# A chunked state-space layer: the state update as three f16 products, and two TensorE steps issued one projection tile later

## The reference, cut to what matters

```python
proj = einsum('bld,pd->blp', hidden_states, in_proj_w)      # gate, x, B, C, dt
xBC  = silu(conv4(hbc))                                     # x, B, C after a causal convolution of 4 taps
dt_p = softplus(dt + dt_bias); dA = exp(dt_p * A); dtx = dt_p[..., None] * x
def step(state, inp):
    state = state * dA_t[..., None, None] + dtx_t[..., None] * B_t[:, :, None, :]
    y_t = einsum('bhpn,bhn->bhp', state, C_t)
y  = ys + x * D
yn = y * rsqrt(mean(y*y) + eps) * norm_weight * silu(gate)  # mean over a group's 512 channels
out = einsum('bli,di->bld', yn, out_proj_w)
```

## Time and profile before

| | |
|---|---|
| median of 3 runs | 4109.71 us (4108.85 to 4112.69) |
| the profiled execution | 4106.15 us, span 4104.3 us |
| L2 attention, first to last slot | 1512 to 3431 us of the span |
| busy in these 1919 us | PE 1824.3, DVE 1624.8, ACT 1312.2, POOL 1496.7 us |
| granted TensorE clock there | 0.99 of full |

### The profile page before, as it was taken

One profiled execution on the slowest core, in us unless ns is written; L12 is line 12 of the kernel. 1 busy time (PEld: TensorE's weight loads), 2 busy tenths in 40 slices (PEclk: granted clock), 3 DMA queues, 4 the chain that ended last, 5 costly groups with the idle time before them and its releaser, 6 DMA issues.

```text
span 4104.3 us, 62802 instructions
## 1 busy us (share of the span) xinstructions
PE 3618.9 (88%) x21250; PEld 1809.9 (44%) x21250; DVE 2896.3 (71%) x4627; ACT 2364.0 (58%) x4071; POOL 2065.2 (50%) x1695
## 2 busy tenths in 40 slices
PE   3889998889888779999999999989999996776799
PEld 1344443223322335555555555545555553343344
DVE  4444335773576458888888888888988886657787
ACT  4533323554456556666666766766666663446665
POOL 4600000000000337787787777778777786546754
PEclk9999997998889989999999999999999997899999
DMA  3200011001100010000000000010000001013000
GB/s 104 68 6 1 1 31 17 1 1 18 36 8 4 10 37 7 25 13 14 25 1 26 13 25 13 8 31 1 25 13 20 11 1 65 1 45 80 16 11 31
DMA packets 58879, 88.92 MB, mean 22 GB/s; under 512 B 11429, under 2 KB 32440, under 8 KB 58548
## 3 DMA queue, kind: packets, MB, share of 16 engines
q1 hardware_dynamic: 57880, 84.15, 7.3%
q10 hardware_dynamic: 672, 0.59, 0.1%
HBM read 71.05 MB, written 6.85 MB: 19 GB/s over the span
## 4 chain that ended last, share of the span: by engine, by line
PE 62%; DVE 14%; issue 8%; ACT 6%; POOL 4%; DVEq 0%; ACTq 0%; DMA 0%; POOLq 0%
PE psum L257 12%; PE psum L259 12%; PE psum L258 12%; PE psum L1388 3%; DVE arena L1550 3%; PE psum L1361 2%; PE psum L2495 2%; PE psum L2483 2%; PE psum L2491 2%; PE psum L2452 2%; PE psum L1372 2%; PE psum L3148 1%; PE psum L3149 1%; DVE x L2177 1%; PE psum L2474 1%
## 5 line engine op out<-in xcount | busy, mean ns | idle before, releaser
L257 PE MATMUL psum<-xt_hi,arena 128*128 128x512 f16 (+1 forms) x1920 | 740.5, 386 | 19.4 <-ACT arena L2005 5.9
L258 PE MATMUL psum<-xt_lo,arena 128*128 128x512 f16 (+1 forms) x1920 | 738.9, 385 | 0.0
L259 PE MATMUL psum<-xt_hi,arena 128*128 128x512 f16 (+1 forms) x1920 | 737.8, 384 | 0.0
L2278 POOL TENSOR_TENSOR arena<-arena 128x1024 f16<-128x1024 f16 x256 | 515.5, 2034 | 49.5 <-DVE arena L2089 32.4
L1501 ACT ACTIVATE arena<-psum 128x512 f32<-128x512 f32 x576 | 320.2, 598 | 276.8 <-PE psum L1372 183.4
L1550 DVE TENSOR_REDUCE arena<-psum 128x1 f32<-128x512 f32 (+3 forms) x608 | 365.3, 654 | 155.3 <-PE psum L1361 154.1
L257 PE MATMUL psum<-arena 128*128 128x512 f16 (+1 forms) x1152 | 418.0, 367 | 57.8 <-DVE arena L2913 26.6
L1306 POOL TENSOR_TENSOR rs<-sd,epsc 128x1 f32<-128x1 f32 x15 | 8.1, 540 | 819.4 <-DVE sd L1598 819.4
L258 PE MATMUL psum<-arena 128*128 128x512 f16 (+1 forms) x1152 | 417.8, 367 | 0.0
L259 PE MATMUL psum<-arena 128*128 128x512 f16 (+1 forms) x1152 | 417.7, 366 | 0.0
L2283 POOL TENSOR_TENSOR arena<-arena 128x512 f16<-128x512 f16 x256 | 314.7, 1248 | 4.8 <-PE psum L2463 4.6
(11 more groups left out here) (363 smaller groups left out, 8340.8 us busy)
## 6 DMA issues: line engine op xcount, KB each, us to landing
arena<-m_wi SPq DMA_DIRECT2D x64, 320.0 KB, 3.0
arena<-m_wo SPq DMA_DIRECT2D x32, 256.0 KB, 2.6
arena<-arena SPq DMA_DIRECT2D x90, 64.0 KB
x<-L_attn_x SPq DMA_DIRECT2D x4, 1024.0 KB, 5.3
arena<-gate_wT SPq DMA_DIRECT2D x16, 224.0 KB, 2.5
arena<-up_wT SPq DMA_DIRECT2D x16, 224.0 KB, 2.5
arena<-down_wT SPq DMA_DIRECT2D x14, 256.0 KB, 2.6
out<-x SPq DMA_DIRECT2D x3, 1024.0 KB, 4.3
```

The lines of the kernel that those rows point to most:

```text
L257: nc.tensor.matmul(out, lh, rh, start=start, stop=False)
L258: nc.tensor.matmul(out, lh, rl, start=False, stop=False)
L259: return nc.tensor.matmul(out, ll, rh, start=False, stop=stop)
L2278: nc.gpsimd.tensor_tensor(m4_ar[:, q], heads[q].broadcast_to([P, HG, P]), m4_le.unsqueeze(1).broadcast_to([P, HG, P]), ALU.mult).then_inc( ...
```

## The change

The state update's f32 matmul becomes three f16 products. For this, B on tokens gets two planes: `b_tokens` makes the high one on ScalarE (a second copy), `b_low` the low one on GpSimd. The stepped x gets two planes: `stepped_high` on ScalarE, `stepped_low` on GpSimd; its steps are scaled by 16, which VectorE divides out again where it adds bank 6 to the state. The copies of the decays for `along` (the two L2283 of GpSimd) become two ScalarE copies, `by_channel`. The update moves out of `chunk` into `state_step`, behind the first projection tile; the turns (`to_tokens`) move behind the second projection tile. VectorE now does `outputs` ahead of `state`. Some semaphores are merged. The core of the diff:

```diff
@@ ScalarE, slot @@
                     tile(act, *nxt, TILES[c][1])
                 square(act, gi, j)
+                if exists(gi, j + 1):
+                    stepped_high(act, *chunk_of(gi, j + 1))
+                if exists(gi, j + 2):
+                    by_channel(act, *chunk_of(gi, j + 2))
                 if nxt:
                     for i in SILU[c]:
                         if i < 5:
@@ b_tokens and the new ScalarE steps @@
             act.wait_ge(m4_xp, n + 1)
             act.wait_ge(m4_sn, n + 1)
-            nc.scalar.activation(m4_bt, psum[:, 3, 0:P], ACT.Copy).then_inc(m4_bk, 1)
+            nc.scalar.activation(m4_bt, psum[:, 3, 0:P], ACT.Copy)
+            nc.scalar.activation(m4_bh, psum[:, 3, 0:P], ACT.Copy).then_inc(m4_bk, 1)
+
+        def stepped_high(act, gi, j):
+            n = gi * CG + j
+            act.wait_ge(m4_x2, n * 2 + 2)
+            act.wait_ge(m4_sn, n + 1)
+            nc.scalar.activation(m4_x2h, m4_x12[:, GF:], ACT.Copy).then_inc(m4_x2hi, 1)
+
+        def by_channel(act, gi, j):
+            n = gi * CG + j
+            act.wait_ge(m4_sp, n * 3 + 2)
+            for q, a in enumerate((m4_ah, m4_al)):
+                heads = a[:, ds(gi * HG + j * HS, HG)].unsqueeze(2)
+                v = nc.scalar.activation(m4_ab[:, q].rearrange("p (h c) -> p h c", c=PS), heads.broadcast_to([P, HG, PS]),
+                                         ACT.Copy)
+            v.then_inc(m4_abk, 1)
@@ VectorE, slot and state @@
                     mask(dve, *chunk_of(gi, j + 1))
+                outputs(dve, ch, gi, j)
                 state(dve, ch, gi, j)
-                outputs(dve, ch, gi, j)
...
-            nc.vector.tensor_tensor(m4_st, m4_st, psum[:, 6, :], ALU.add).then_inc(m4_sk, 1)
+            nc.vector.scalar_tensor_tensor(out=m4_st, in0=psum[:, 6, :], scalar=1.0 / X2S, in1=m4_st, op0=ALU.mult,
+                                           op1=ALU.add).then_inc(m4_sk, 1)
@@ GpSimd @@
-                pool.wait_ge(m4_sp, n * 3 + 2)
-                alone(pool)
-                for q in range(2):
-                    nc.gpsimd.tensor_tensor(m4_ab[:, q].rearrange("p (h c) -> p h c", c=PS),
-                                            heads[q].broadcast_to([P, HG, PS]),
-                                            m4_on[:, 0:PS].unsqueeze(1).broadcast_to([P, HG, PS]),
-                                            ALU.mult).then_inc(m4_ak, 1)
+
+            def b_low(gi, j):
+                n = gi * CG + j
+                pool.wait_ge(m4_bk, n + 2)
+                pool.wait_ge(m4_sn, n + 1)
+                nc.gpsimd.tensor_tensor(m4_bl, m4_bt, m4_bh, ALU.subtract)
+
+            def stepped_low(gi, j):
+                n = gi * CG + j
+                pool.wait_ge(m4_x2hi, n + 1)
+                nc.gpsimd.tensor_tensor(m4_x2l, m4_x12[:, GF:], m4_x2h, ALU.subtract).then_inc(m4_x2lo, 1)
@@ GpSimd, slot @@
                 nc.gpsimd.tensor_tensor(sg, m4_xc[x % 2][:, 2:6, tok], sg, ALU.mult).then_inc(m4_yn, 1)
+                if exists(gi, j + 1):
+                    b_low(*chunk_of(gi, j + 1))
                 pool.wait_ge(m4_qk, n + 2)
...
                 nc.gpsimd.tensor_tensor(m4_sq[:, 0, :], m4_sq[:, 0, :], m4_sq[:, 1, :], ALU.add).then_inc(m4_qs, 1)
+                if exists(gi, j + 1):
+                    stepped_low(*chunk_of(gi, j + 1))
@@ TensorE, slot @@
                 if nxt:
                     in_proj(pe, *nxt, TILES[c][0])
+                state_step(pe, gi, j)
+                if nxt:
+                    in_proj(pe, *nxt, TILES[c][1])
                 if exists(gi, j + 1):
                     to_tokens(pe, *chunk_of(gi, j + 1))
-                if nxt:
-                    in_proj(pe, *nxt, TILES[c][1])
@@ TensorE, chunk @@
             last.then_inc(m4_ia, 1)
-            pe.wait_ge(m4_x2, n * 2 + 2)
-            nc.tensor.matmul(psum[:, 6, :], m4_bt, m4_x12[:, GF:], start=True, stop=True).then_inc(m4_sn, 1)
+
+        def state_step(pe, gi, j):
+            n = gi * CG + j
+            pe.wait_ge(m4_x2lo, n + 1)
+            three(pe, psum[:, 6, :], m4_bh, m4_bl, m4_x2h, m4_x2l, True, True).then_inc(m4_sn, 1)
```

More of the change, by code:

```diff
@@ L692, in build @@
         m4_ab = carve(117832, [2, GF], F16)
+        m4_x2h = carve(137376, [GF], F16)
+        m4_x2l = carve(138400, [GF], F16)
+        m4_bh = carve(136864, [P], F16)
+        m4_bl = carve(137120, [P], F16)
+        X2S = 16.0
         m4_e1 = carve(119880, [HG, P], F32)
@@ L731, in build @@
         m4_pi = sem("m4_pi")
-        m4_cpk = sem("m4_cpk")
-        m4_nwk = sem("m4_nwk")
+        m4_prk = sem("m4_prk")
         m4_whi = sem("m4_whi")
@@ L748, in build @@
         m4_xd = sem("m4_xd")
-        m4_dpk = sem("m4_dpk")
         m4_bk = sem("m4_bk")
         m4_x2 = sem("m4_x2")
+        m4_x2hi = sem("m4_x2hi")
+        m4_x2lo = sem("m4_x2lo")
+        m4_abk = sem("m4_abk")
         m4_ii = sem("m4_ii")
@@ L823, in build @@
         q7_done = sem("q7_done")
-        z7_open = sem("z7_open")
         z7_moved = sem("z7_moved")
@@ L1828, in group @@
                 if not is_last(gi):
-                    sp.wait_ge(m4_nwk, gi + 1)
+                    sp.wait_ge(m4_prk, gi * 3 + 3)
                     sp.dma_start(m4_pn.unsqueeze(1), A["m4_par"][:, ds(gi + 1, 1), :]).then_inc(m4_pi, 16)
@@ L1921, in act_l2_attn @@
                 convolved(act, 0, 0, i)
+            act.wait_ge(m4_tv, 4 + 3)
+            by_channel(act, 0, 0)
             decays(act, 0, 0)
@@ L1924, in act_l2_attn @@
             b_tokens(act, 0, 0)
+            stepped_high(act, 0, 0)
+            by_channel(act, 0, 1)
             skipped(act, 0, 0)
@@ L1963, in slot @@
                 if x == 0 and c == 0:
-                    act.wait_ge(m4_nwk, gi + 1)
+                    act.wait_ge(m4_prk, gi * 3 + 3)
                     act.wait_ge(m4_op, gi * CG + 1)
@@ L1992, in before @@
                 act.wait_ge(m4_cy, gi * HF + (x + 1))
-                act.wait_ge(m4_cpk, gi + 1)
+                act.wait_ge(m4_prk, gi * 3 + 1)
                 if not is_first(gi, x * 4 - 4):
@@ L2039, in skipped @@
             if j == 0:
-                act.wait_ge(m4_dpk, gi + 1)
+                act.wait_ge(m4_prk, gi * 3 + 2)
             xs = m4_xc[j // 4 % 2]
@@ L2091, in dve_l2_attn @@
                 dve.wait_ge(m4_ta, 5 * n + 5)
-                nc.vector.tensor_tensor(m4_dt2[:, hc], m4_dtp[:, hc], m4_v, ALU.mult).then_inc(m4_tv, 1)
+                nc.vector.scalar_tensor_tensor(out=m4_dt2[:, hc], in0=m4_dtp[:, hc], scalar=X2S, in1=m4_v,
+                                               op0=ALU.mult, op1=ALU.mult).then_inc(m4_tv, 1)
             dve.wait_ge(m4_tv, 8)
@@ L2159, in conv_params @@
             nc.vector.tensor_scalar(m4_t3, m4_pn[:, 0:CT * KC].rearrange("p (i k) -> p i k", k=KC)[:, :, KC - 1], 1.0 / WS,
-                                    None, ALU.mult).then_inc(m4_cpk, 1)
-            dve.wait_ge(m4_cpk, gi + 1)
+                                    None, ALU.mult).then_inc(m4_prk, 1)
+            dve.wait_ge(m4_prk, gi * 3 + 1)
         def late_params(dve, gi):
-            nc.vector.tensor_scalar(m4_nw, m4_pn[:, CT * (KC + 1) + 4:], WS, None, ALU.mult).then_inc(m4_nwk, 1)
-            dve.wait_ge(m4_nwk, gi + 1)
+            nc.vector.tensor_scalar(m4_nw, m4_pn[:, CT * (KC + 1) + 4:], WS, None, ALU.mult).then_inc(m4_prk, 1)
+            dve.wait_ge(m4_prk, gi * 3 + 3)
         def skip_params(dve, gi):
@@ L2170, in skip_params @@
             nc.vector.tensor_scalar(m4_dp4, m4_pn[:, CT * (KC + 1):CT * (KC + 1) + 4], 1.0, None,
-                                    ALU.mult).then_inc(m4_dpk, 1)
+                                    ALU.mult).then_inc(m4_prk, 1)
         def convolve(dve, ch, gi, x, i):
@@ L2315, in pool_l2_attn @@
             spread(0, 1)
+            b_low(0, 0)
+            stepped_low(0, 0)
             def group(gi):
@@ L2447, in between @@
             n = gi * CG + j
-            pe.wait_ge(m4_ak, n * 4 + 2)
+            pe.wait_ge(m4_ak, n * 2 + 2)
             for q in range(2):
@@ L2458, in along @@
             n = gi * CG + j
-            pe.wait_ge(m4_ak, n * 4 + 4)
+            pe.wait_ge(m4_abk, n + 1)
             pe.wait_ge(m4_ek, n * 3 + 3)
@@ L2759, in act_late @@
                 elif what == "w_open":
-                    act.wait_ge(w7_o, u + 1)
+                    act.wait_ge(w7_o, 2 + u + 1)
                     if u >= 2:
@@ L3035, in sp_zeros7 @@
             sp.dma_start(sh7, A["shifts"]).then_inc(z7_moved, 16)
-            sp.wait_ge(z7_open, 2)
+            sp.wait_ge(w7_o, 2)
             sp.dma_start(zeros7_gu, zf7[0:2 * KT].bitcast(F32)).then_inc(z7_moved, 16)
@@ L3047, in dve_zeros7 @@
                 nc.vector.tensor_scalar(zf7[a:b, 0:8 * w], zu7[a:b, 0:w, :].rearrange("p a b -> p (a b)"), 1.0, scale, ALU.add,
-                                        ALU.mult).then_inc(z7_open, 1)
+                                        ALU.mult).then_inc(w7_o, 1)
         def loads7(i):
```

## The result

The changed kernel takes 4367.6 us (median of 4 runs, 4366.11 to 4376.9), the one before 4110.86 beside it: ratio 1.0629, 95% interval 1.0611 to 1.0648. It is slower, as forecast, but by 257 us and not by 175: above the range.

The account below looks back on a forecast made before the run. TensorE bound the kernel before; loops through ScalarE were to bind after. Seven groups +155, the last +4.8, +6.5, +6.5 and +2, sum +175: 4106.15 became 4281, with the median 3.6 higher 4284 us; range 4190 to 4345.

Parts of the forecast that it names:

- TensorE's own work: State update on TensorE: three f16 matmuls cost 0.65 us for 0.96, saving 0.31 a slot, 40 us in 128 slots.
- The moves and ScalarE's queue: Turns end at T + 6.58, ScalarE's work queues behind `b_tokens`, `gated` over at T + 14.66; stage 1 64.05 against 57.58.
- these loops: Paths back to the next T: by `add_out` T + 17.55, by `along` T + 17.06, both above TensorE's 15.23.
- The rival in which TensorE stays the bound: Faster, 4027 or 4060 us, if `gated` is over by T + 12.3 and both loops stay under 15.23; chance 0.10.
- T: Start of the slot's first projection tile on TensorE, from which times are counted; period before the change 15.54 us.
- VectorE's chain is then over at about T + 16, under the loops: VectorE, standing still until the turns at T + 6.5, ends its list from `stepped` to the second convolution about T + 16.
- Inside the longer period: VectorE's late `variance` holds up `b_dot_c` by about 1 us, inside the longer slot period.
- Slots with pieces: ScalarE's pair of weight pieces adds 1.35 us to both loops; stages 0, 2, 3 come to 66.2, 67.35, 68.65.
- The clock: Rival: new waits before T make TensorE's clock fall, a tile costing up to 2.59 us more; 4335 and more, chance 0.08.
- The turns' wait for the state nearly gone: Sign: the turns' waits on TensorE for the state, 43.1 us in all before, nearly vanish, mostly covered by the second tile.
- Neither product is needed before the next slot's T + 2.6: GpSimd's two new subtractions, 128 and 512 columns, the larger 1.40 us, are not needed before the next slot's T + 2.6.

Follow-up runs that it names:

- e2: The changed kernel with the old places: three f16 products inside `chunk`, turns between the two tiles, `state` ahead of `outputs`; 4115.96 us, ratio 1.0000.
- e7: The changed kernel with `by_channel` ahead of `b_tokens` on ScalarE and `stepped_low` behind `root` on GpSimd; 4304.42 us, ratio 1.0477.
- e6: The kernel before with only the turns moved behind the second projection tile; 4283.91 us, ratio 1.0427.
- e1: The kernel before with the moves but no planes: f32 state update behind the first tile, turns behind the second, `outputs` ahead of `state`; 4316.86 us, ratio 1.0471.
- e11: The kernel before with VectorE making the next group's parameters at the end of stage 2, not at the start of stage 3; 4094.32 us, ratio 0.9948.
- e4: The changed kernel with VectorE's `variance` directly behind `stepped`; 4400.46 us, ratio 1.0673.
- e5: The changed kernel with the weight pieces ahead of `b_tokens` on ScalarE and between `outputs` and `state` on VectorE; 4350.77 us, ratio 1.0590.
- e12: e2 with VectorE's stage 2 pieces all in slot 3, the next group's parameters there too, ScalarE's pieces 2 and 3 behind `gated`; 4074.97 us, ratio 0.9917.
- e3: The changed kernel with `by_channel` moved ahead of `b_tokens` on ScalarE; 4364.41 us, ratio 1.0586.
- e9: e2 with only the two VectorE pieces of stage 2's slot 3 moved from behind `stepped` to behind `masked`; 4121.78 us, ratio 1.0015.

## Why the prediction had the direction and the plain slots right and was short by a third

**TensorE's own work: right.** Three f16 products save 0.31 us a slot (e2: 15.24 against 15.55).

**The moves and ScalarE's queue: right for stage 1.** Turns, `gated`, `decays`, `along` and the first tile came within 0.3 us of their forecast times, the stage at 63.6 against 64.05. E7 confirms it from the other side: what relieves these loops gives 2.4 us of the stage back. The rival in which TensorE stays the bound fell; its condition (`gated` at T + 12.3) was missed by 2.1 us. Stage 2 (67.9 against 67.35) was luck: slot 2 takes 18.2 where 16.6 was forecast, and the other three are each 0.3 to 0.4 shorter than forecast.

**"VectorE's chain is then over at about T + 16, under the loops": right as a statement, wrong as a reason to leave it out.** Without ScalarE's new work (e6, e1) the late turns still cost 4.1 and 3.6 us a stage. "Inside the longer period", said of the late variance, holds for the plain slots of the changed kernel, where `b_dot_c` waits 0.2 to 0.6 us; in e6 it costs 0.47 us in slots 0 and 1. In the slots with pieces it fails (below). In slot 3 VectorE's loop costs 1.8 us (the row of e6), by way of the second tile's bank, which I had not counted as one of VectorE's loops.

**"Slots with pieces": the step that failed.** Of the 82 us that are missing, 69 lie in seven times the difference of the table's two rows (9.85 us a group), and about 7 in the last group. I took a piece as 1.35 us more on ScalarE's path and nothing else, and the late variance as about 1 us inside the longer period. The runs show two waits of TensorE in its place: the output projection's for the pieces themselves (3.71 us in each group, 0.96 before), and `b_dot_c`'s for a variance that stands behind VectorE's pieces (3.09, 1.28 and 2.97 us in each group, 0.83 before). Stage 0's slot 1 was forecast at 18.9 and takes 24.4. Its rows, TensorE:

```profile
1829.43 0.66 PE L2516 MATMUL psum<-ident,x 128*128 128x128 f32 x4 [1.03 <-DVE arena L2264]
...
1834.03 0.60 PE L257 MATMUL psum<-arena 128*128 128x512 f16 x1 [3.71 <-DVE arena L1870]
...
1835.28 0.63 PE L257 MATMUL psum<-arena 128*128 128x512 f16 x1
```

ScalarE and VectorE, the last pieces of the output weights:

```profile
1831.74 1.32 ACT L1859 ACTIVATE arena<-arena 128x512 f16<-128x512 f32 x2
```

```profile
1821.92 4.01 DVE L1870 SCALAR_TENSOR_TENSOR arena<-arena 128x512 f16<-128x512 f32 x2
...
1832.48 1.41 DVE L1870 SCALAR_TENSOR_TENSOR arena<-arena 128x512 f16<-128x512 f32 x2 [0.83 <-ACT arena L1859]
```

The output projection needs these pieces, and they are made by both engines behind the turned B. Moving the turns moved them too, to 1833.89, and the projection waits 3.71 us; in the kernel before the same wait is 0.96. On top come 1.03 us at the turns, since slot 0's pieces (4.01 us on VectorE) stand ahead of the state. I asked of ScalarE's queue what is behind the turned B, and not who waits on TensorE for each thing in it. Stage 3 is short by the same kind of step: slots of 22.4, 20.4, 14.0 and 17.8 against 20.05, 18.9, 15.2 and 14.5. In slot 0 the state's wait was put at 1.6 us and is 2.08:

```profile
2014.16 0.66 PE L2516 MATMUL psum<-ident,arena 128*128 128x128 f32 x4 [2.08 <-DVE arena L2264]
...
2015.73 0.63 PE L257 MATMUL psum<-arena 128*128 128x512 f16 x1
...
2021.49 0.49 PE L2485 MATMUL psum<-arena 128*128 128x128 f32 x2 [1.28 <-DVE arena L2281]
...
2040.44 0.49 PE L2485 MATMUL psum<-arena 128*128 128x128 f32 x2 [2.97 <-DVE arena L2281]
```

and the variance is late again, by 1.28 here and by 2.97 in slot 1. The turns' wait in slot 0 was 3.33 us before, and e11 shows that it came from the parameters, not from the update. The third of these waits is in stage 2's slot 2, TensorE and then VectorE:

```profile
1985.90 0.46 PE L2485 MATMUL psum<-arena 128*128 128x128 f32 x2 [3.09 <-ACT arena L2027]
```

```profile
1981.51 1.56 DVE L1870 SCALAR_TENSOR_TENSOR arena<-arena 128x640 f16<-128x640 f32 x2 [0.86 <-ACT arena L1856]
1982.98 2.74 DVE L2207 SCALAR_TENSOR_TENSOR arena<-arena 128x512 f32<-128x512 f32 x3
1985.65 0.15 DVE L2281 TENSOR_SCALAR arena<-psum 128x1 f32<-128x1 f32 x1
```

Two pieces and a convolution stand between `stepped` and the variance, and `b_dot_c` follows the variance by 0.10 us. E4, which lifts the variance over both, shortens these three slots by 1.7, 1.2 and 2.4 us. The waits can't simply be added to the loss: e5 and e4 show that others grow where these are taken away. Slot 3 ends a group; 3.3 us are missing in the forecast of it, and `chunk` of the next group waits there:

```profile
2075.90 1.28 PE L2525 MATMUL psum<-x,arena 128*128 128x128 f32 x8 [2.50 <-issue]
```

No releaser is named for these 2.50 us (0.70 to 1.25 in the kernel before), and what the wait is for stays open. It is 2.3 to 2.6 us in e6 as well, so it comes with the late turns. The matmuls behind it run slower too (1.28 against 1.05).

**The clock: a share that I had given 0.08.** Behind the waits of 3.71 and 2.08 us the 512-column matmuls take 0.63 instead of 0.38 us (rows above), 0.216 more between starts. In the attention's projection and output matmuls such records (over 0.5 us) number 45 before and 207 after: 162 x 0.216 = 35 us of the 257, and the forecast's sum has no term for them, so up to 35 of the missing 82 us are the clock's. In e12 they number 46. The waits of about 1 us in stage 1 cost no clock (1.00). The Trainium skill ("TensorE: Matmul & The Clock Gate", section "HAM oscillation — how this bites in real kernels") says that waits between bursts of matmuls can bring the throttle back; by that rule the forecast could be 4350 or more. The traces agree in the direction, for slots with long waits and not for the others, and not each time: behind the wait of 2.97 us above the matmuls stay at 0.38, and behind the wait of 3.3 us of the earlier trace rows they fall to 0.63 in four of the groups 1 to 6 and stay at 0.38 in two. So the length of one wait does not tell what it costs in clock. E6 has 164 such records, 119 more than before (26 us): it is the late turns that bring most of them.

**"The turns' wait for the state nearly gone": wrong.** It fell from 43.1 to 26.7 us only. **"Neither product is needed before the next slot's T + 2.6": wrong for GpSimd's queue.** The low plane of the stepped x stands ahead of the low plane of the gated y there, and so on the way to `add_out` (e3, e7).

So of the 258 us that the ratio of 1.0629 makes, the turns alone are 175 (e6, with some 20 that only e6 has), the later update and `outputs` ahead of `state` some 19 more (e1, which lacks e6's 20, so their own share is nearer 40), and the planes on top of late turns 64 (e1 to after), of which e7 takes back 62 by two orders. With the turns in place the same planes cost nothing (e2). The parts are not additive: the planes are dear only where the turns start ScalarE late.

## What to carry to other kernels

A step moved one tile later delays all that is queued behind its consumer on every engine. Go through each engine's queue behind it, pieces of weights and small reductions too, and ask for every entry who waits for it. In a kernel with 0 to 2 us of slack a slot, judge new work in the slots with extra duties first: a stage of plain slots was forecast within 0.5 us, and of the 9.85 us missing in a group 60% lay in stage 3 and 38% in stage 0. When a wait is attributed to a step, look a slot back at what stood ahead of that step (e9), and at whether a constant job stands there that could go into an idle gap (e11).
